# Neighbour sweeps of a two-layer graph kernel: one split unit more, its remainders shared between GpSimd and VectorE, and four ring buffers

## What is computed

```
h  = relu(layernorm(x));   x = x + (adj.T @ h) / colsum(adj)[:, None]
h  = relu(layernorm(x))
x1 = swish((adj @ h)  @ W + b)
x2 = swish((adj @ x1) @ W + b);   return x + x2
```

## Time and profile before

| | |
|---|---|
| three executions, median | 719.79 us |
| the profiled execution | 717.73 us, of which the span of the trace is 715.7 us |
| TensorE matmul busy | 643.0 us (90%) |
| VectorE busy | 510.0 us (71%) |
| ScalarE busy | 299.2 us (42%) |
| GpSimd busy | 565.7 us (79%) |
| mean granted TensorE clock | 0.964 |
| moved from and to HBM | 199 MB |

### The profile page before, as it was taken

How to read it: one execution, slowest core, us unless ns; L and a number is a source line. 1 busy time by engine, 2 the same in 40 slices (tenths; PEclk the granted TensorE clock), 3 DMA queues, 4 the chain that set the end, 5 groups by cost and what they waited for, 6 DMA issues and landing times.

```text
span 715.7 us, 6437 instructions
## 1 busy us (share of the span) xinstructions
PE 643.0 (90%) x2212; PEld 407.0 (57%) x2212; DVE 510.0 (71%) x516; ACT 299.2 (42%) x345; POOL 565.7 (79%) x254
## 2 busy tenths in 40 slices
PE   4487899899899889989999999999999899899995
PEld 2144565565565456556566566566566556566563
DVE  3673778868968764967787677777677867767861
ACT  2372332362362352454544444445444334344341
POOL 2228876978668566899899898998998788798792
PEclk9888999999999986999999999999999999999999
DMA  8985878897878999999999999918999999999941
GB/s 280 296 312 184 307 282 298 297 335 266 291 281 306 335 223 342 260 278 304 307 327 346 290 333 346 292 45 162 314 317 345 258 321 328 308 295 345 281 103 29
DMA packets 155759, 199.78 MB, mean 279 GB/s; under 512 B 5456, under 2 KB 138832, under 8 KB 155728
## 3 DMA queue, kind: packets, MB, share of 16 engines
q1 hardware_dynamic: 87728, 134.23, 60.9%
q10 hardware_dynamic: 68000, 65.15, 33.3%
HBM read 197.26 MB, written 2.10 MB: 279 GB/s over the span
## 4 chain that ended last, share of the span: by engine, by line
PE 50%; POOL 20%; DMA 10%; ACT 8%; DVE 6%; ACTq 3%; issue 1%; SPq 1%; DVEq 0%
PE dg L319 16%; POOL at_lo L664 10%; POOL a_lo L652 8%; DMA raw<-in_adj_dram 8%; PE dg L329 8%; PE dg L325 6%; PE dg L326 6%; PE m_ps L270 5%; ACTq L209 3%; ACT a_hi L381 2%; DVE turned L558 2%; PE m_ps L279 2%; PE m_ps L336 2%; DMA h<-in_x_dram 2%; ACT at_hi L409 2%; PE m_ps L273 2%
## 5 line engine op out<-in xcount | busy, mean ns | idle before, releaser
L664 POOL TENSOR_TENSOR at_lo<-turned,at_hi 128x1024 fp32r<-128x1024 f32 x160 | 379.4, 2409 | 49.6 <-ACT at_hi L409 49.4
L558 DVE STREAM_TRANSPOSE turned<-raw 128x1024 f32<-128x1024 f32 x256 | 302.5, 1222 | 115.8 <-PE dg L319 88.6
L409 ACT ACTIVATE at_hi<-turned 128x1024 fp32r<-128x1024 f32 x160 | 167.4, 1057 | 205.8 <-DVE turned L558 138.1
L652 POOL TENSOR_TENSOR a_lo<-raw,a_hi 128x2048 fp32r<-128x2048 f32 x33 | 150.0, 4554 | 68.3 <-ACT a_hi L381 68.3
L319 PE MATMUL dg<-turned,f_w 128*128 128x512 f32 x384 | 182.0, 597 | 0.0
L515 DVE TENSOR_TENSOR dg<-raw,dg 128x2048 f32<-128x2048 f32 x60 | 137.6, 2293 | 59.2 <-DMA raw<-in_adj_dram 58.2
L325 PE MATMUL dg<-at_hi,f_hi 128*128 128x512 f32 x320 | 162.9, 509 | 6.0 <-ACT at_hi L409 6.0
L270 PE MATMUL m_ps<-raw,h 128*128 128x512 f32 x248 | 116.0, 614 | 19.4 <-DMA raw<-in_adj_dram 19.4
L326 PE MATMUL dg<-at_hi,f_lo 128*128 128x512 f32 x320 | 128.0, 400 | 0.0
L381 ACT ACTIVATE a_hi<-raw 128x2048 fp32r<-128x2048 f32 x33 | 63.0, 1913 | 140.0 <-DMA raw<-in_adj_dram 140.0
L329 PE MATMUL dg<-at_lo,f_hi 128*128 128x512 f32 x320 | 105.3, 411 | 16.8 <-POOL at_lo L664 16.5
(11 more groups left out here) (47 smaller groups left out, 250.3 us busy)
## 6 DMA issues: line engine op xcount, KB each, us to landing
raw<-in_adj_dram SPq DMA_DIRECT2D x64, 1024.0 KB, 6.4
raw<-in_adj_dram ACTq DMA_DIRECT2D x120, 512.0 KB, 12.7
raw<-in_adj_dram SPq DMA_DIRECT2D x120, 512.0 KB, 10.3
x<-in_x_dram SPq DMA_DIRECT2D x16, 128.0 KB, 6.1
out_dram<-zs ACTq DMA_DIRECT2D x16, 128.0 KB, 9.2
h<-in_x_dram SPq DMA_DIRECT2D x1, 768.0 KB, 9.8
h<-in_x_dram SPq DMA_DIRECT2D x1, 256.0 KB, 3.2
w<-in_L_gnn_W_dram ACTq DMA_DIRECT2D x1, 64.0 KB, 2.9
```

Of the source, the lines that this page charges most:

```text
L409: act.activation(at_hi[:, s % RING3], turned[:, unit % TURN], ACT.Copy).then_inc(hi3_done, 1)
L558: dve.transpose(dst, src).then_inc(t3_done, 1)
L652: pool.tensor_tensor(a_lo[:, s % RING1], raw1[:, v % RAW1], a_hi[:, s % RING1].bitcast(f32), ALU.subtract).then_inc(lo1_done, 1)
L664: pool.tensor_tensor(at_lo[:, s % RING3], turned[:, unit % TURN], at_hi[:, s % RING3].bitcast(f32), ALU.subtract).then_inc(lo3_done, 1)
```

## The change

Four edits. `WHOLE3` has five units, j = 0, 3, 6, 9, 12, so eleven units of a group are split. Of the eleven remainders VectorE makes two, j = 5 and 13 (`DVE_LO3`), each right behind its transposition of the next unit; GpSimd makes nine. The semaphore of the remainders is split in two accordingly. The rings `at_hi` and `at_lo` have four slots. SBUF is laid out anew to make room: the rings move ahead, the unused `gap` shrinks from 3072 to 512 columns, and `u` shrinks by two tiles.

```diff
-WHOLE3 = (0, 3, 6, 8, 11, 14)
+WHOLE3 = (0, 3, 6, 9, 12)
+DVE_LO3 = (5, 13)
-RING3 = 3
+RING3 = 4
...
+        def by_dve(unit):
+            return PIECES[unit // QU][1] * QU + unit % QU in DVE_LO3
+
+        def wait_lo3(eng, unit):
+
+            mine = [s for s in splits3 if by_dve(s) == by_dve(unit)]
+            eng.wait_ge(lo3_dve if by_dve(unit) else lo3_pool, mine.index(unit) + 1)
+
+        def lo3(eng, unit):
+            s = split3(unit)
+            eng.wait_ge(hi3_done, s + 1)
+            return eng.tensor_tensor(at_lo[:, s % RING3], turned[:, unit % TURN], at_hi[:, s % RING3].bitcast(f32),
+                                     ALU.subtract)
...
@@ turned_free
-                    eng.wait_ge(lo3_done, split3(back) + 1)
+                    wait_lo3(eng, back)
@@ m3
-                    pe.wait_ge(lo3_done, split3(unit) + 1)
+                    wait_lo3(pe, unit)
@@ vector
                 turn3(unit)
+                if unit > 0 and by_dve(unit - 1):
+                    lo3(dve, unit - 1).then_inc(lo3_dve, 1)
@@ gpsimd
-                if not whole3(unit):
-                    lo3(unit)
+                if not whole3(unit) and not by_dve(unit):
+                    lo3(pool, unit).then_inc(lo3_pool, 1)
```

More of the change, by code:

```diff
@@ L89, in build @@
         degs = sb("degs", [P, QC], into=sweep1)
-        u = sb("u", [P, QT, P], into=sweep1)
+        u = sb("u", [P, QT - UC, P], into=sweep1)
         sweep1.close()
@@ L96, in build @@
         f3_w = sb("f3_w", [P, UC * len(WHOLE3), P], into=sweep2)
+        at_hi = sb("at_hi", [P, RING3, UC, GROUP], f32r, into=sweep2)
+        at_lo = sb("at_lo", [P, RING3, UC, GROUP], f32r, into=sweep2)
         nT = sb("nT", [P, 2, QC], into=sweep2)
         zs = sb("zs", [P, 2, QT, P], into=sweep2)
-        at_hi = sb("at_hi", [P, RING3, UC, GROUP], f32r, into=sweep2)
-        at_lo = sb("at_lo", [P, RING3, UC, GROUP], f32r, into=sweep2)
-        gap = sb("gap", [P, 3 * 1024], into=sweep2)
+        gap = sb("gap", [P, 512], into=sweep2)
         raw3[0] = sb("raw3_0", [P, GB, BC], into=sweep2)
@@ L132, in build @@
         t3_done = sem("t3_done")
-        hi3_done, lo3_done = sem("hi3_done"), sem("lo3_done")
+        hi3_done = sem("hi3_done")
+        lo3_pool, lo3_dve = sem("lo3_pool"), sem("lo3_dve")
         m3_done = sem("m3_done")
@@ L659, in lo_h2 @@
                                    f2_hi[:, tiles].bitcast(f32), ALU.subtract).then_inc(h2_ready, 1)
[L661 to L665, removed]
             def lo_x1(r):
```

## The result

The changed kernel took 728.8 us (median of four executions, 728.27 to 734.4) against 718.91 for the kernel before (now four executions too, 714.59 to 722.94). The ratio is 1.0135, with a 95% interval of 1.0072 to 1.0198: slower by 1.35%. The profiled execution took 729.13 us; its span is 727.3 us, 11.6 more than before.

What follows compares the result with a forecast made beforehand. TensorE and GpSimd bounded the kernel before; with the change GpSimd would, at 25.7 to 25.8 us a group. 717.73 + 6 (first neighbour sweep) + 3.5 (second) + 1.5 (first pair) = 728.7, 729 us; range 710 to 738.

Steps and rivals of the forecast that it cites:

- GpSimd's gap: Before GpSimd's j = 7, once a group: idle 3.4 us, as VectorE's waiting j = 5 subtraction delays the transposition of j = 7.
- the walk: One group followed from the end of GpSimd's j = 11: 21.3 + 1.0 + 3.4 = 25.7 to 25.8 us.
- rival (a): At j = 5 VectorE gets in before GpSimd's j = 4 in about every second group: about 721 us; chance 0.17.
- VectorE's subtractions: Line 176 on VectorE, 32 instructions: mean near 2.5 us, those of j = 5 near 3.0, waiting for GpSimd's instruction.
- First neighbour sweep: Four pairs of groups at 53.5 us on average against 52.03 before: +1.5 each, +6 us.
- Second neighbour sweep: Pairs with residual additions and stores: 57 us against 55.99 and 55.49, +1 for the last stretch; +3.5, between 0 and +7.
- rival (c): VectorE's subtraction also waits for high parts while DMA issues hold ScalarE's queue: 12 to 15 us more, about 742; chance 0.08.
- First pair: The stretch up to 337 us: same pattern among other waits, +1.5 us, by the measure of a later pair.
- The ring at nothing: Four slots remove ScalarE's 38.9 us of waits for line 329, costed at nothing: earlier high parts are only queued for GpSimd.
- the 2 us that a pair lost before at bias and silu: Time beyond TensorE's 50.2 us a pair, where TensorE waits for bias, silu, then `at_lo`, `f_lo`, `at_lo` on GpSimd.

Runs made afterwards that it cites:

- the later place: The changed kernel with VectorE's two subtractions one transposition later (j = 5 behind the transposition of j = 7, 13 behind 15): 709.48 us, ratio 0.9837.
- the PSUM operand: The changed kernel with VectorE's subtraction reading its second operand from PSUM from unit 32 on, so these remainders are wrong: 710.8 us, ratio 0.9868.
- the last two runs: The changed kernel, VectorE's subtractions one transposition later, stores by SyncE, six whole units: 0, 3, 6, 8, 11, 14 took 710.13 us; 0, 3, 6, 9, 12, 14 took 696.91.

## Why the prediction was right, point by point

**GpSimd's gap.** The step that decided was the walk through one group from GpSimd's j = 11. It gave a gap of 3.4 us and the trace has 3.41; it gave 25.8 us a group and 53.7 a pair, and the trace has 53.68. VectorE missed GpSimd's j = 4 by 0.3 us in group 3 (0.4 predicted). In the first sweep it missed by as little in groups 2 and 8 only, and by 1.0 to 1.2 in the others. In groups 4 and 6 an issue of two loads holds ScalarE for 2.4 us (at 384.56 and at 438.2) and the high part comes 0.7 us late; in 5, 7 and 9 VectorE's j = 13 of the group before went in ahead of GpSimd's j = 11, and GpSimd comes to j = 4 0.8 us earlier than in the walk. Both kept VectorE further from winning the race of rival (a). What does not depend on the miss is the end: VectorE is done 1.08 us after GpSimd's instruction. The runs with the later place and with the PSUM operand show both halves of the mechanism.

**VectorE's subtractions were cheaper than I said.** I expected a mean near 2.5 us, near 3.0 for j = 5; the 32 took 2.08 on average, those of j = 5 2.27, since VectorE came later in GpSimd's instruction than in the walk. VectorE was busy 46.3 us a pair, 23.1 a group, where I had 24.5. This changes nothing in the sum, as VectorE's end is tied to GpSimd's.

**First neighbour sweep.** Predicted +6 us for four stretches; 213.99 against 208.13, +5.9.

**Second neighbour sweep.** Predicted +3.5 (0 to +7): 166.7 against 160.5 by the start of `xw`, +6.2. The sign and the range held; the size was a little over half of what was measured. I took 57, 57 and +1 for the last; it was 55.9, 58.3 and +3.5. What I mis-sized is what I had set aside as rival (c), VectorE waiting for a high part that ScalarE's held queue delivers late: 10.3 us of waits after 540 us. The run with all remainders on GpSimd, at the same GpSimd pace, is 5.7 us faster in these stretches, and that is the only place where it differs. I had also taken 1 to 2 us off because VectorE's j = 5 would once get ahead of GpSimd's j = 4 behind a store: it did so only in group 15, in the last stretch, and the gap before j = 7 was 3.41 or 3.42 us in groups 10 to 14 all the same.

**First pair.** Predicted +1.5; the first `xw` was 0.4 us earlier than before. The neighbour sweep itself began 1.9 us earlier (260.7 against 262.6), a point that varied from 260.3 to 264.5 over the kernels of this study, none of which changed the sweep before it but for feature splits and places in SBUF. So 1.5 us are there from the start of the sweep on, and a start that fell well hides them.

**Cancelling errors.** The two misses (+2.7 and -1.9) nearly cancel in the sum, 11.0 predicted and 11.6 measured in the span. The total is closer than its parts.

**The ring at nothing.** Right: 0.0% alone, and within 3 us inside the change. Its worth appears only when GpSimd is no longer the bound (0.4 us a pair).

**What I passed over.** I took the 2 us that a pair lost before at bias and silu as gone and not needed, since GpSimd bounds. That was right for the change, but the change's best part was there: the new places of the whole units remove nearly all of that loss, as the last two runs show (52.0 against 50.3 us a pair); by the chain it is the one at j = 9. By these runs the change brought a gain of 1.6 us a pair and hid it behind a gap of twice 3.4.

## What to carry to other kernels

When work is moved to a less busy engine, follow what stands behind it in that engine's queue: an instruction that may have to wait belongs behind the one whose result the other engine needs next, here one place later, which was worth 2.7% of the kernel (728.8 to 709.5). Walk one period of the steady state with durations from rows, starting at the engine that is last, and see whether it closes on itself; the sum of busy times (23.3 and 23.9 here, both under the 24.2 before) said faster. Then look at which unit of a pattern meets the side chain (bias, silu, split): its place can be worth more than one unit more or less.

## What the runs showed that I had not expected

**A waiting VectorE instruction can lose its turn.** In the trace before and in all 32 instructions of the change, no VectorE instruction waited longer than to the end of the GpSimd instruction that was running: none lasted over 3.3 us. In the run with j = 4 on VectorE two of 32 lasted 5.00 us: issued at 398.09, passed by GpSimd at 399.60. Two more, of 3.47 and 3.48 us, were issued 0.05 us before the end of GpSimd's subtraction and passed by the next one. In the run with all remainders on GpSimd it happened at each of three residual additions. VectorE and GpSimd:

```profile
616.07 5.29 DVE L592 TENSOR_TENSOR zs<-zs,x 128x1024 f32<-128x1024 f32 x1
```
```profile
615.57 4.71 POOL L176 TENSOR_TENSOR at_lo<-turned,at_hi 128x1024 fp32r<-128x1024 f32 x2
```

Here VectorE comes 0.50 us after GpSimd has begun, and GpSimd does this and the next subtraction without a pause or a stretch (4.71 us for two). In the trace before, the same addition came 0.52 us after GpSimd had begun, with GpSimd's next high part ready as well, and was next. The Trainium skill, page SBUF — State Buffer, section Who interferes with whom, says that issue order decides who blocks; the cases of 5.00 and 5.29 us do not agree with that. What decided between them stays open: I made no run on it.

**The lock is a matter of the operand's memory.** The same subtraction of 128x1024 elements took 1.18 to 1.22 us beside a busy GpSimd with one operand in PSUM, and up to 3.3 us with both in SBUF in the change; the transposition, with one SBUF operand, never took more than 1.25 us.

**DMA issues on a compute engine's queue.** A pair of loads issued by ScalarE took less than 1 us in 26 of 56 cases of the change, mostly 0.86, and 5.89 us behind the second store. Moving the 16 stores to SyncE took 9.7 us off the changed kernel (728.8 to 719.1).
